# Pool makes the attention mask tile by tile, and the attention half is ordered anew around VectorE

## What is computed

```python
def _L0_gnn_ref(h, adj, W, a):            # h = layernorm(x), adj int32 16x512x512
    Wh = einsum('bni,oi->bno', h, W)
    si, sj = Wh @ a[0, :128], Wh @ a[0, 128:]
    e = leaky_relu(si[:, :, None] + sj[:, None, :], 0.2)
    attention = softmax(where(adj > 0, e, -9e15), axis=-1)
    return elu(einsum('bij,bjo->bio', attention, Wh))

def _L0_ffn_ref(x, Wr, br, W1, b1, W2, b2, gamma, beta):
    # router: mean over the tokens @ Wr + br, two softmaxes with a capacity scale, top 2 of 8
    h = gelu(einsum('nd,edf->enf', xf, W1) + b1)          # F = 256
    y = einsum('enf,efd->end', h, W2) + b2
    return layer_norm(out + x, gamma, beta)               # out = gated sum of the two experts

x = x + gnn(layernorm(x), adj, W, a)
x = x + ffn(layernorm(x), ...)
```

## Time and profile before

| | |
|---|---|
| median of 3 runs | 361.11 us (358.62 to 361.22) |
| the profiled execution | 358.76 us |
| its span in the trace | 357.0 us |
| PE, busy share of the span | 78% |
| DVE | 79% |
| ACT | 62% |
| POOL | 65% |

### The profile page before, as it was taken

One profiled execution on the slowest core, in us unless ns is written; L12 is line 12 of the kernel. 1 busy time (PEld: TensorE's weight loads), 2 busy tenths in 40 slices (PEclk: granted clock), 3 DMA queues, 4 the chain that ended last, 5 costly groups with the idle time before them and its releaser, 6 DMA issues.

```text
span 357.0 us, 7414 instructions
## 1 busy us (share of the span) xinstructions
PE 278.7 (78%) x1797; PEld 243.3 (68%) x1797; DVE 282.9 (79%) x792; ACT 222.0 (62%) x463; POOL 230.3 (65%) x421
## 2 busy tenths in 40 slices
PE   7598869398399386697786948259899999999990
PEld 3387748388298286586676838236898999989990
DVE  3998999959959979779897793740498988989975
ACT  3658867648739756956984884234765747567430
POOL 4857989989989989889889492600442533425341
PEclk9879978969969988988996996756999999999996
DMA  7734224044053042153044100024834544545411
GB/s 252 272 148 151 77 101 176 1 179 160 18 176 139 38 176 106 70 176 129 19 149 133 46 2 30 29 93 129 281 119 148 184 148 162 185 147 181 164 39 60
DMA packets 24696, 44.53 MB, mean 125 GB/s; under 512 B 2624, under 2 KB 12256, under 8 KB 22496
## 3 DMA queue, kind: packets, MB, share of 16 engines
q1 hardware_dynamic: 24672, 44.27, 35.3%
HBM read 27.48 MB, written 4.20 MB: 89 GB/s over the span
## 4 chain that ended last, share of the span: by engine, by line
POOL 38%; PE 34%; issue 14%; DVE 8%; DMA 2%; POOLq 2%; ACT 1%; DVEq 0%; SPq 0%; ACTq 0%
PE banks L1208 14%; POOL rstd L401 9%; POOL x2s L439 9%; PE banks L1193 5%; POOL x1b_all L441 4%; PE banks L1195 4%; PE banks L1194 4%; POOL sums L399 4%; PE banks L1116 2%; POOL sums L391 2%; POOL sums L395 2%; DVE x2s L627 2%; POOL sums L388 2%; PE banks L1102 1%; POOL sums L387 1%
## 5 line engine op out<-in xcount | busy, mean ns | idle before, releaser
L1116 PE MATMUL banks<-whx,prob_t 128*128 128x129 f32 x512 | 72.8, 300 | 0.7 <-ACT prob_t L924 0.6
L1116 PEld LDWEIGHTS banks<-whx,prob_t 128*128 128x128 f32 x512 | 70.1, 218 | 1.5 <-ACT prob_t L924 1.5
L924 ACT ACTIVATE prob_t<-banks 128x512 f32<-128x512 f32 x64 | 35.6, 590 | 44.5 <-PE banks L1102 44.5
L575 DVE SCALAR_TENSOR_TENSOR logit<-masked_dst,shift_pos,leaky 128x512 f32<-128x512 f32 x64 | 46.3, 776 | 0.6 <-ACT leaky L897 0.2
L897 ACT ACTIVATE leaky<-masked_dst,shift_neg 128x512 f32<-128x512 f32 x64 | 42.6, 717 | 6.5 <-DVE shift_neg L564 6.5
L1102 PE MATMUL banks<-ident,logit 128*128 128x128 f32 x256 | 43.9, 313 | 3.0 <-DVE logit L575 2.1
L439 POOL TENSOR_SCALAR x2s<-x1s,nm,rstd 128x128 f32<-128x128 f32 x56 | 41.7, 755 | 3.0 <-POOL rstd L401 3.0
L1093 PE MATMUL banks<-ident,x2s 128*128 128x128 f32 x64 | 13.9, 356 | 34.8 <-POOL x2s L439 33.4
L401 POOL TENSOR_TENSOR rstd<-sums,minus_half 128x4 f32<-128x4 f32 x30 | 38.6, 1288 | 2.4
L542 DVE CUSTOM_DVE_ANT_0 masked_dst<-mask,banks 128x512 f32<-128x512 bf16 x64 | 40.0, 680 | 0.2 <-issue 0.2
L493 POOL TENSOR_SCALAR veps<-mv 128x4 f32<-128x4 f32 x16 | 3.8, 237 | 56.3 <-DVE mv L814 56.3
(11 more groups left out here) (137 smaller groups left out, 628.5 us busy)
## 6 DMA issues: line engine op xcount, KB each, us to landing
adj_sb<-in_adj_dram SPq DMA_DIRECT2D x16, 1024.0 KB, 4.9
w_pair<-w_parts SPq DMA_DIRECT2D x32, 256.0 KB, 2.4
x_all<-in_x_dram SPq DMA_DIRECT2D x16, 256.0 KB, 4.9
x_all<-x2s SPq DMA_DIRECT2D x16, 256.0 KB, 2.3
w2r<-in_L_ffn_W_dram SPq DMA_DIRECT2D x32, 128.0 KB, 2.3
out_dram<-prob_t SPq DMA_DIRECT2D x16, 256.0 KB, 2.0
adj_sb<-in_L_ffn_W_dram SPq DMA_DIRECT2D x1, 1024.0 KB, 5.5
adj_sb<-b_spread SPq DMA_DIRECT2D x1, 1024.0 KB, 5.2
```

Source lines behind the costliest of these rows:

```text
L575: nc.vector.scalar_tensor_tensor(out=logit[:, t, :], in0=masked_dst[:, t, :], scalar=shift_pos[:, t:t + 1], in1=leaky[:, t, :], op0=ALU.ad ...
L924: nc.scalar.activation(prob_t[:, t, :], lt_ps[t % 2], ACT.Exp).then_inc(s_prob, 1)
L1116: last = nc.tensor.matmul(into[:, 0:D + 1], prob_t[:, t, c * P:(c + 1) * P], whx[par][:, c, 1:WHX], start=(c == 0), stop=(c == T - 1))
```

## The change

What is computed stays. All of it concerns the attention half and the passage to the experts, but for the beta addition:

- The layout is "(t p)": partition p holds tokens p, 128 + p and so on. x is loaded twice, once for the attention (`x_rows`) and once for the residual.
- Norm 1 is no longer applied to x. The weights are centred once at the start, TensorE transposes the raw x, and the scale 1/std is applied when `whx` is copied out, in four instructions instead of one.
- The destination term is made from `whx` by four products with a broadcast column (`spread_dst`) instead of one of 512 columns.
- Pool makes the mask, one tile at a time, and the row shifts. Its two norms become one chain over both, `norms`, for batch n+2 and batch n-3. The four `x2s` tiles leave Pool: VectorE does two, ScalarE two.
- The beta addition (`add_beta`) moves from the attention half to Pool's loop in the expert half, in place on `x1_all`.
- The orders of all engines are laid anew. VectorE's is masked maxima 2 and 3, residual of batch n-2, two `x2s` tiles, statistics, then logits interleaved with the next batch's masked maxima 0 and 1. Residual and norm 2 come a step later than before.
- The last x2 transposes follow the attention loop. The two halves of w1's split and the first two splits of x2t are placed elsewhere. The first batch's expert weights are copied by VectorE and Pool instead of by DMA.

```diff
-    x_dram = x.rearrange("b (p t) d -> b p t d", t=T)
+    x_dram = x.rearrange("b (t p) d -> b p t d", t=T)
...
@@ sync: step
+                if in_range(half, n + 3) and past(half, n + 3, 2):
+                    load_adj(half, n + 3)
+                if in_range(half, n + 4) and past(half, n + 4, 2):
+                    load_rows(half, n + 4)
+                if in_range(half, n + 3) and past(half, n + 3, 2):
+                    load_x(half, n + 3)
+                if in_range(half, n - 2, END - 2):
+                    keep_x2(half, n - 2)
...
@@ gpsimd
+            def norms(half, n):
...
+                nc.gpsimd.tensor_tensor(sums[:, 1, kinds, :], bn[:, kinds, :, 1], bn[:, kinds, :, 4],
+                                        ALU.subtract).then_inc(s_norm, 1)
...
+                nc.gpsimd.tensor_tensor(rstd[:, kinds, :], sums[:, 1, kinds, :],
+                                        minus_half[:].unsqueeze(1).to_broadcast([P, 2, T])[:, kinds, :],
+                                        ALU.pow).then_inc(s_norm, 1)
+                if second:
+                    pool.wait_ge(s_norm, base + 7)
+                    pool.wait_ge(s_n2, 3 * b2n + 2)
+                    nc.gpsimd.tensor_tensor(nb2[par][:], nm2[:], rstd[:, 1, :], ALU.mult).then_inc(s_n2, 1)
+
+            def make_mask(half, n, t):
+
+                b, h, par = batch_at(half, n)
+                if t == 0:
+                    pool.wait_ge(s_adj[par], 16 * h + 16)
+                if past(half, b, 1):
+                    pool.wait_ge(s_md, T * (b - 1) + t + 1)
                 waits_met(pool)
-                for t in range(T):
-                    tile = slice(t * D, (t + 1) * D)
-                    nc.gpsimd.tensor_scalar(x2s[par][:, tile], x1s[par][:, tile], nm2[:, t:t + 1], rstd2[:, t:t + 1],
-                                            ALU.add, ALU.mult).then_inc(s_x2, 1)
...
+                nc.gpsimd.tensor_scalar(mask[:, t, :], adj_sb[par][:, t, :], 0.0, -MASKED, ALU.is_le,
+                                        ALU.mult).then_inc(s_mask, 1)
+
+            def row_shifts(half, n):
...
+                nc.gpsimd.tensor_scalar(src_alpha[:], src, ALPHA, 0.0, ALU.mult, ALU.add).then_inc(s_shift, 1)
+                pool.wait_ge(s_md, T * b + T)
+                nc.gpsimd.tensor_tensor(z_max[:], src, dst_max[:], ALU.add).then_inc(s_shift, 1)
+                pool.wait_ge(s_shift, base + 2)
+                waits_met(pool)
+                nc.gpsimd.tensor_scalar(z_alpha[:], z_max[:], ALPHA, 0.0, ALU.mult, ALU.add).then_inc(s_shift, 1)
+                nc.gpsimd.tensor_scalar(z_pos[:], z_max[:], 0.0, 1.0 - ALPHA, ALU.max, ALU.mult).then_inc(s_shift, 1)
+                pool.wait_ge(s_shift, base + 4)
+                nc.gpsimd.tensor_tensor(row_max[:], z_pos[:], z_alpha[:], ALU.add).then_inc(s_shift, 1)
+                pool.wait_ge(s_shift, base + 5)
+                nc.gpsimd.tensor_tensor(shift_neg[:], src_alpha[:], row_max[:], ALU.subtract).then_inc(s_shift, 1)
+                nc.gpsimd.tensor_tensor(shift_pos[:], src, row_max[:], ALU.subtract).then_inc(s_shift, 1)
...
+            def step(half, n):
+                if in_range(half, n):
+                    make_mask(half, n, 0)
...
+                if in_range(half, n + 2, END - 1 + NORM_LAG):
+                    norms(half, n + 2)
+                if in_range(half, n):
+                    row_shifts(half, n)
...
@@ gpsimd: step2, behind the power
+                if in_range(half, n):
+                    add_beta(half, n)
...
@@ vector
-                nc.vector.tensor_scalar(mask[:].rearrange("p t (c k) -> p t c k", c=T),
-                                        adj_sb[par][:].rearrange("p t (k c) -> p t c k", c=T),
-                                        0.0, -MASKED, ALU.is_le, ALU.mult).then_inc(s_mask, 1)
...
+                if in_range(half, n):
+                    masked_max(half, n, 2)
+                if in_range(half, n):
+                    masked_max(half, n, 3)
+                if in_range(half, n - 2, B - 2):
+                    residual_pos(half, n - 2)
+                if in_range(half, n - 2, B - 2):
+                    residual_neg(half, n - 2)
+                if in_range(half, n - 3, END - 1):
+                    scale_x2(half, n - 3)
                 if in_range(half, n + 3):
                     stats1(half, n + 3)
...
+                if in_range(half, n - 2, END - 1):
+                    stats2(half, n - 2)
+                if in_range(half, n):
+                    logits(half, n, 0)
+                if in_range(half, n - 1, B - 2):
                     invert_sums(half, n - 1)
                 if in_range(half, n):
+                    logits(half, n, 1)
                 if in_range(half, n + 1):
+                    masked_max(half, n + 1, 0)
+                if in_range(half, n):
+                    logits(half, n, 2)
+                if in_range(half, n + 1):
+                    masked_max(half, n + 1, 1)
+                if in_range(half, n):
+                    logits(half, n, 3)
...
+            aggregate2(0, B - 1, (B - 1) % 2)
+            split_x2t_lo(0, 0)
+            split_x2t_lo(0, 1)
+            scale_x2_end(B - 1)
...
+            e = dve.value_load(top_idx[0:1, 0:1], min_val=0, max_val=E - 1)
+            nc.vector.tensor_copy(w1_pair[0][:, 0], w1_parts[:, e]).then_inc(s_pick[0], 1)
...
@@ scalar
-                    nc.scalar.activation(xn[:, t, :], x_all[:, b, t * D:(t + 1) * D], ACT.Identity,
-                                         bias=nb1[par][:, t:t + 1], scale=rstd1[par][:, t:t + 1]).then_inc(s_xn, 1)
...
+                for t in range(T):
+                    nc.scalar.activation(whx[par][:, t, 0:D + 2], wh_ps[:, t, 0:D + 2], ACT.Copy,
+                                         scale=rstd12[par][:, 0, t:t + 1]).then_inc(s_wh, 1)
...
+                if in_range(half, n):
+                    probs(half, n, 1)
+                if in_range(half, n - 2, END - 1):
+                    scale_x2(half, n - 2)
+                if in_range(half, n):
+                    probs(half, n, 2)
+                if in_range(half, n):
+                    probs(half, n, 3)
...
@@ tensor
-                nc.tensor.matmul(dst_ps, dst_weights[:], xnt[:], start=True, stop=True).then_inc(s_dst, 1)
...
+                for t in range(T):
+                    last = nc.tensor.matmul(dst_ps[:, t * P:(t + 1) * P], whx[par][:, t, 0:1].to_broadcast([P, P]),
+                                            ident[:], start=True, stop=True)
+                last.then_inc(s_dst, 1)
```

More of the change, by code:

```diff
@@ L315, in _ @@
             sp.dma_start(b2_sb[:], b2).then_inc(s_rw, 16)
-            load_x(0, 3)
             def step(half, n):
                 if isinstance(half, int) and n == B - 2:
[L320 to L331, removed]
+                    sp.wait_ge(s_mask, T * (B - 1))
@@ L467, in _ @@
-            pipeline(pool, step, FIRST, LAST, LEAD, LAG)
-            keep_x1b(B - 2)
-            keep_x1b(B - 1)
-            for b in range(2):
-                pool.wait_ge(s_hi, b + 1)
-                nc.gpsimd.tensor_tensor(x2t_lo[b][:], x2t_all[:, b, :], x2t_hi[b][:].bitcast(F32),
-                                        ALU.subtract).then_inc(s_x2lo, 1)
+                base, src = 7 * b, whx[par][:, :, 1]
+                if past(half, b, 1):
+                    pool.wait_ge(s_logit, T * b)
+                    pool.wait_ge(s_leaky, T * b)
@@ L475, in _, with add_beta @@
+            def add_beta(half, n):
+                b, h, par = batch_at(half, n)
+                nc.gpsimd.tensor_tensor(x1_all[:, b, :].rearrange("p (t d) -> p t d", t=T),
+                                        x1_all[:, b, :].rearrange("p (t d) -> p t d", t=T),
+                                        beta_less_one[:].unsqueeze(1).to_broadcast([P, T, D]), ALU.add).then_inc(s_x1b, 1)
+            for par in range(2):
+                pool.wait_ge(s_x2k[par], 16 * (B // 2))
             pool.wait_ge(s_b2mix, 16)
@@ new lines, in logits @@
+            def logits(half, n, t):
+                b, h, par = batch_at(half, n)
+                if t == 0:
+                    dve.wait_ge(s_shift, 7 * b + 7)
+                dve.wait_ge(s_leaky, T * b + t + 1)
+                if past(half, b, 1):
+                    dve.wait_ge(s_lt, T * (b - 1) + t + 1)
+                nc.vector.scalar_tensor_tensor(out=logit[:, t, :], in0=masked_dst[:, t, :],
+                                               scalar=shift_pos[:, t:t + 1], in1=leaky[:, t, :],
+                                               op0=ALU.add, op1=ALU.max).then_inc(s_logit, 1)
@@ L875, in copy_xnt @@
                 act.wait_ge(s_xt_ps, b + 1)
-                if not isinstance(half, int) or b >= 1:
+                if past(half, b, 1):
                     act.wait_ge(s_wh_ps, b)
@@ new lines, in scale_x2 @@
+            def scale_x2(half, n):
+                b, h, par = batch_at(half, n)
+                if past(half, b, 2):
```

(24 more changed lines are left out.)

755 lines of the change are left out of this document (378 added, 377 removed).

## The result

The changed kernel takes 395.1 us (394.6 to 396.5) against 359.9 in the same session: 1.099 of the time before, 95% interval 1.092 to 1.107. The forecast was 350, in a range of 342 to 358, and a gain. The trace of after spans 392.8 us, 35.8 more than before.

What follows compares the result with a forecast made beforehand. Pool was taken to bound the attention half and TensorE the expert half. Terms of -16.5 + 1 - 7 + 13.5 = -9 us took the profiled 358.8 to 349.8, forecast as 350, range 342 to 358.

Steps and rivals of the forecast that it cites:

- The first half's bound and Pool's own work: Attention half: Pool paces it; its own work per step falls from 9.3 to 8.4 us.
- The mask tile: Pool, attention half: a 512-column mask tile costs 0.62 us, priced from L425; four are 2.5 us per step.
- The far bound: Pool's mask tile: at most 1.28 us, from the two-input 512-element operation; four are 5.1 us.
- Contention: Attention half: Pool loses 70% of VectorE's 4.8 us of port-taking work, 3.3 us per step.
- Rival B: Pool's mask is dear: each 0.1 us per tile adds 6 us, gain gone beyond 0.77; mostly 360 to 375; chance 0.32.
- C: Expert half stays on TensorE, as VectorE's tiles win the port or x2b slips later: 336.5 us; chance 0.16.
- D: Nothing measurable: other engines' queues set the attention step at 12.2 us, gains and losses cancel, 358 us; chance 0.12.
- The rest of the sum: Whole kernel: attention -16.5, start +1, between the halves -7, expert half +13.5, together -9 us.
- VectorE and the others: Attention half: VectorE's step becomes 11.2 us, close behind Pool's 11.7; ScalarE stays near 9 and TensorE has slack.
- Start: Before the first logits: weights centred first and masks after two norms; logits at 18.5 instead of 17.67, +1 us.
- Between the halves: Passage to experts: x2s tiles 3 us less, first weights copied without DMA 2 less, transposes 2 less; -7 us.
- Expert half: finish waits for a second Pool operation, add_beta; VectorE becomes the bound; 0.9 us per batch, +13.5 us.

Runs made afterwards that it cites:

- the cheap mask: The kernel after with Pool's mask as (adj - 1) x 2^53 by add and multiply instead of compare and multiply: 343.2 us, 0.962 of before.
- the run that turns it round: The kernel after with mask by add and multiply, add_beta beside the statistics, and x_rows loaded ahead of adj on SP's queue: 332.3 us, 0.929 of before.
- two kernels: The kernel after with Pool's mask by add and multiply (343.2 us), and the kernel after with the mask back on VectorE (347.2 us).

## Why the prediction was wrong, point by point

- **The first half's bound and Pool's own work:** right but for one term. Norms of 4.0, shifts of 1.9 (measured 1.6) and a power over 8 columns of 1.86 (measured 1.65) were right within some tenths, and Pool did stay the bound. With the cheap mask its own work is 8.3 us; I had 8.4.
- **The mask tile:** the step that failed. I extended L425, an add and a multiply, to a compare and a multiply because both are operations with one input and two immediates. The number 0.62 was exact for the operation it came from: the add form takes 0.618. The compare takes 1.92. The term was 2.5 us a step and measured 7.7; that the term turned the sign is shown by the run with the add. The far bound was wrong too: I took the dearest 512-column row of another kind as a ceiling, and nothing made it one.
- **Contention:** 3.3 us forecast. After has about 0.6: its undisturbed operations, added from the first batches, come to 13.4 of 14.07. With the cheap mask it is near 1.7 of a step of 10.87, after 0.85 of idling is taken off. So the step had two errors of opposite sign, +5.2 and -2.7, and the second softened the first. I took the loss as a share of VectorE's port-taking time; beside the masks the traces show it only where a tile of one engine starts while the other engine reads (see the last section).
- **Rival B** was the right mechanism at the wrong price. It had the gain gone at 0.77 us a tile and 390 at 1.28. Measured, two tiles at 0.62 and two at 1.92, 1.27 on average, take 356.1, 0.996 of before: the break-even lies near 1.3, above all because most of the 3.3 us of contention in my step isn't there. By its 6 us for each 0.1 us of tile, 1.92 would have been 428; it is 395.1. It had a chance of 0.32, and its range ended at 390 because the tile price ended at 1.28.
- **Rivals C and D:** `finish` did wait for both Pool operations, so the expert half left TensorE (against C). A step of 12.2 us set by the other engines' loop (D) isn't there: two kernels run at 11.0.
- **The rest of the sum** is tested by the run with the add, whose mask costs what I assumed: 343.2 against 350. It is within the range, but terms cancel. Against the forecast the start is 4.8 us longer, the 15 steps are 10.7 shorter (10.99 instead of 11.7), the passage between the halves is 2.2 longer and the expert half 2.9 shorter. That the total comes so near is in part luck.
- **VectorE and the others:** 11.2 forecast as the next bound, 11.0 measured once Pool is out of the way. But VectorE idles there 1.1 to 1.5 us of a step at one place and is busy 79% of it, so the agreement of the numbers is luck.
- **Start:** +1 forecast, +10.8. Of it 5.0 is the four compares, by the run with the add, and 1.5 SP's queue, by the run that turns it round (with the cheap mask). The rest, about 4.3, I put down to the longer serial chain, which no run splits: the weights come first (Pool's first sum starts at 6.22 instead of 4.24), then norms and masks one after another on Pool before anything can overlap. I counted only the norms in front of the masks, and not the masks and the third norm ahead of the first shifts.
- **Between the halves:** -7 forecast, -4.4. The last `x2s` tiles fell from 4.88 to 1.11, as expected. But the copies of the first weights start 1.1 us after the index, and then the router's own chain is the later one: small products on its results stand ahead of the first expert product in TensorE's order and end at 266.8.
- **Expert half:** right in place and mechanism, and nearly in size: `finish` 2.9 (forecast 3.1), step 7.09 (7.2), +10.3 (13.5).

## What to carry to other kernels

A price from one row holds for the operation in that row, not for its class; where a new operation has no row of its own, a far bound from rows of other kinds is no ceiling, and the range should say so. When an engine that sets the pace is given new work, measure that one operation by itself before ordering everything around it: here one operation code decided between 10% slower and 4% faster. And work that two engines contend for goes beside the other's instructions that don't take part, as the beta addition does beside the statistics.

## What the runs showed of the hardware

- A Pool `tensor_scalar` with a compare costs three times one with an add: 1.92 against 0.62 us for 128x512, for int32 or f32 in and bf16 or f32 out. The Trainium skill's page "GPSIMD Engine Reference" (section 3, Performance versus the Vector engine) gives about 769 ns for 512 elements in the best loop. The add is below that figure and the compare two and a half times it.
- A conversion from int32 to bf16 costs Pool nothing measurable: 0.61 us as a copy, 0.62 with add and multiply, and 0.62 too for f32 to f32.
- A slow Pool operation doesn't disturb VectorE for as long as it runs. In the kernel after, beside mask tiles of undisturbed length, a logits tile that starts within the first 0.42 us of a mask tile waits until 0.42 us after the mask's start, and one that starts later doesn't wait. Three mask tiles and the logits tiles beside them, in short windows:

```profile
154.09 1.92 POOL L474 TENSOR_SCALAR mask<-adj_sb 128x512 bf16<-128x512 int32 x1
154.77 0.75 DVE L618 SCALAR_TENSOR_TENSOR logit<-masked_dst,shift_pos,leaky 128x512 f32<-128x512 f32 x1
...
155.98 1.92 POOL L474 TENSOR_SCALAR mask<-adj_sb 128x512 bf16<-128x512 int32 x1
156.04 1.09 DVE L618 SCALAR_TENSOR_TENSOR logit<-masked_dst,shift_pos,leaky 128x512 f32<-128x512 f32 x1
...
166.11 1.93 POOL L474 TENSOR_SCALAR mask<-adj_sb 128x512 bf16<-128x512 int32 x1
166.18 1.08 DVE L618 SCALAR_TENSOR_TENSOR logit<-masked_dst,shift_pos,leaky 128x512 f32<-128x512 f32 x1
```

  The first starts 0.68 us into its mask and keeps 0.75 us. The others start 0.06 and 0.07 into theirs and take 0.35 longer. With the add form, a mask of 0.62 us, a logits tile that starts 0.02 us into one (at 120.02 in that trace) takes 1.14, so the wait ends at the same 0.42 us. A two-input Pool operation of 1.38 us in the expert half holds up a `finish` tile until about 1.2 us after its start. So the time held isn't the length of the operation; that it is the time in which Pool reads its input fits all three, but is my inference. A mask that finds a logits tile under way is itself longer, up to 2.5 us.

  The Trainium skill's page "SBUF — State Buffer" (section Who interferes with whom) has the pair of ports held for the whole instruction. By that the logits tile at 154.77 would have waited until 156.01, 1.2 us. The trace of after doesn't agree, while the beta addition in the expert half is close to what the page says.
